# The last phase's down projection by seven block products instead of eight

## The chip, the cores and the metric

The kernel runs on one core of one Trainium2 chip. The metric is device time in microseconds from launch to end; smaller is better.

## The reference, cut to what matters

Four batches ("tiles" here) of 512 tokens, 512 features. Three blocks follow each other, each with a residual:

```
x = x + 0.5 * ffn(layernorm(x))       # hidden 2048
x = x + scan_layer(layernorm(x))      # z = x W^T, gated scan over tokens, 4 decays, layernorm
x = x + 0.5 * ffn(layernorm(x))       # the same ffn weights

ffn(x):  gate = x Wg^T;  up = x Wu^T;  h = silu(gate) * up;  return h Wd^T     # all fp32
```

The down projection `h Wd^T` is [512 tokens x 2048] by [2048 x 512] for each tile.

## The kernel before, in words

**Precision.** Every fp32 product is made of three matmuls in the fp32r format (`three`, L1567 to 1571): both operands are split into a high part (a cast by ACT) and a low part (value minus high part, by DVE), and high x high, high x low and low x high are summed in PSUM.

**Phases.** The eight ffn passes (four tiles, two ffns) are done two at a time, in four phases `p` of two token tiles each, called tile 0 and tile 1 of the phase. Phase 0 also reads and splits all weights and keeps the split ones in DRAM (`gu_kept`, `dn_kept`); later phases fetch them. Phases 1 and 2 carry the scan layer beside them. Phase 3 (`LAST` in the change) only has an ffn.

**Sets.** A phase has 16 sets, one for each hidden tile pair member; gate and up of both token tiles are made by seven products (`prod1` to `prod7`, six matmuls of 512 columns each) of sums of operands, Winograd's form of Strassen's scheme. Over two sets (even, odd) the hidden rows 2q and 2q+1 of tile 0 and tile 1 come out (`gated11`, `gated21`, `gated12`, `gated22`, L1069 to 1096). DVE joins the products (`c11`, `c22`, `c12`, L1048 to 1067); ACT copies partial results out of PSUM and applies silu.

**Down projection.** Tile 0's goes beside the sets: in set si `down0(si - 2)`, half of it (`down0_begin`) after prod6, half (`down0_end`) after prod4; steps 14 and 15 follow set 15. A step is 4 token groups x `three` = 12 matmuls of 512 columns. Tile 1's hidden rows stay in `hid1`, and its 16 steps `down1(p, m)` (L1697) follow in the "window" at the end of the phase, from `zx`, a ring of four rows that `d1_hi` (ACT, L785) and `d1_lo` (DVE, L1321) fill. Weights stand in `dn`, a ring of four (hi and lo of one inner tile, 512 KB), fetched by `fetch_dn` (L426) on SP's queue.

**The order** of every engine is written out by hand; all waits are on semaphores. In phase 0 POOL makes four sums of the gate and up weights of a set (`sums`, L941), ACT and DVE split them (`gu_hi_a`, `gu_lo_a` and so on) and the down weights (`dn_hi_of`, `dn_lo_of`), one set ahead of their use; SP stores them (`keep_a`, `keep_b`, `keep_dn`). In the windows of phases 0 to 2 DVE also normalises and transposes the next phase's input (`norm_x`, `blocks_x`, with POOL's `place_second` and the sums `t_of`, L1462 to 1519), between its `d1_lo` steps.

```
                d1_lo(p, 0)
                d1_lo(p, 1)
                d1_lo(p, 2)          # L1464 to 1466: DVE's window begins
```

**The end.** `add_y1` (DVE, L1333) adds half of each PSUM bank to `x_tok`, and SP stores each 256 KB unit (L570).

Of the kernel before, what the change touches and what calls it, by code (L numbers as in the profile page):

```python
# [44 lines left out]


def macaron_kernel(nc, x_in, w_ffn_in, w_scan_in, lam_logit_in, eta_in, gamma_in, beta_in, out):
# [10 lines left out]
    DN = 4  # L58
    assert tokens == 512 and D == 512 and DT == ST == 4 and HT == 16 and tiles == 4 and K == 4

    with ExitStack() as ctx:
# [10 lines left out]
        xt = sb("xt", [P, 7, 2, 2, tokens], F32R)  # L72
        zx = sb("zx", [P, 2, DT, tokens], F32R)
# [4 lines left out]
        dn = sb("dn", [P, DN, 2, D], F32R)  # L78
# [49 lines left out]
        dn_kept = nc.dram_tensor("dn_kept", [HT, P, 2, D], F32).ap()  # L128
# [9 lines left out]
        d1_ps = [ps_a, ps_b, ps_c, aux]  # L138
        first_turn_ps = [ps_d[0], ps_d[1], ps_d[2], ps_d[3], ps_a, ps_b, ps_d[2], ps_d[3]]
# [131 lines left out]
        zw_loaded = sem("zw_loaded")  # L271
        x_stored = sem("x_stored")
# [18 lines left out]
        d1_last = sem("d1_last")  # L291
        turned_x = sem("turned_x")
# [29 lines left out]
        zw_lo = sem("zw_lo")  # L322
        y0_added, y1_added = sem("y0_added"), sem("y1_added")
# [29 lines left out]
        def _(sp):  # L353
# [120 lines left out]
            for k in range(2, SETS):  # L474
# [32 lines left out]
            keep_dn(15)  # L507
            sp.wait_ge(dn_stored[2], 16 * 4)
# [17 lines left out]
            for p in range(1, PH):  # L526
                for si in range(SETS):
# [18 lines left out]
                    fetch_dn(32 * p + si - 2 + DN)  # L546
                    if g + 2 < SETS * PH:
                        fetch_b(g + 2)
                    if beside and si == 15:
                        load_back(p, 0, 0)  # L550
                        load_back(p, 0, 1)
                for n in range(32 * p + 14, 32 * p + 32):
# [9 lines left out]
                    if p == 2 and m in (8, 10, 12, 14) or p == 3 and m in (4, 6, 8, 10):  # L562
                        sp.wait_ge(y0_added, 4 * p + 4)
                        store_unit(2 * (p - 2), (m - (8 if p == 2 else 4)) // 2)
# [3 lines left out]
            for q in range(ST):  # L568
                sp.wait_ge(y1_added, 4 * (PH - 1) + q + 1)
                sp.dma_start(out_v[3, :, q, :], x_tok[:, 3 * ST + q, :]).then_inc(out_stored, 16)  # L570
            sp.wait_ge(out_stored, 16 * 13)

        @block.scalar
        def _(act):
# [120 lines left out]
            def dn_hi_of(h):  # L695
# [3 lines left out]
                act.copy(dn[:, h % DN, 0, :], dn_raw[:, h % 2, :]).then_inc(dn_hi, 1)  # L699
# [85 lines left out]
            def d1_hi(p, m):  # L785
                wait(act, d_done, 32 * p + 16 + m - 4 + 1 if m >= 4 else 32 * p)
                if m < 4 and p == 0:
                    act.wait_ge(plain_done, 8)
# [3 lines left out]
                act.copy(zx[:, 0, m % 4, :], hid1[:, m, :]).then_inc(d1hi_ready, 1)  # L792

# [64 lines left out]
            for p in range(PH):  # L858
# [3 lines left out]
                for si in range(2, SETS):  # L862
# [45 lines left out]
                g = SETS * p + SETS - 1  # L908
                d1_hi(p, 0)
# [30 lines left out]
        def _(pool):  # L940
            def sums(k):  # L941
# [9 lines left out]
                pool.tensor_tensor(w[:, 7, :], w[:, 4, :], w[:, 1, :], ALU.subtract).then_inc(sums_ready, 1)  # L951

# [58 lines left out]
            for k in range(2, SETS + 1):  # L1011
# [3 lines left out]
                sums(k)  # L1015
                if k == 11:
# [30 lines left out]
        def _(dve):  # L1047
# [21 lines left out]
            def gated11(g):  # L1069
# [4 lines left out]
                dve.tensor_tensor(v, v, sg("11"), ALU.mult).then_inc(hid11_done, 1)  # L1074
# [16 lines left out]
            def gated21(g):  # L1091
# [3 lines left out]
                dve.tensor_tensor(sg("21"), sg("21"), chain_bank(g % SETS)[:, :], ALU.mult  # L1095
# [340 lines left out]
            def one_set(p, si):  # L1436
# [12 lines left out]
                before_c12(p, si)  # L1449
                c12(g)  # L1450
                if up:
                    gated12(g)
                    lo0(g, 1)
# [102 lines left out]
            for p in range(PH):  # L1556
# [6 lines left out]
                window(p)  # L1563

        @block.tensor
        def _(pe):
# [101 lines left out]
            def down0(p, h, q):  # L1668
# [3 lines left out]
                return three(ps_d[q][:, :], hid0[:, h % 2, 0, a], hid0[:, h % 2, 1, a], dn[:, s, 0, :],  # L1672
                             dn[:, s, 1, :], h == 0, h == HT - 1)
# [23 lines left out]
            def down1(p, m):  # L1697
# [4 lines left out]
                for q in range(ST):  # L1702
# [10 lines left out]
                    last = three(d1_ps[q][:, :], zx[:, 0, m % 4, a], zx[:, 1, m % 4, a], dn[:, s, 0, :],  # L1713
# [198 lines left out]
```

## Time and profile before

| | us |
|---|---|
| median of 3 runs (1021.63 to 1021.70) | 1021.67 |
| span of the profiled execution | 1020.2 |
| PE busy in it | 1014.4 |
| DVE / ACT / POOL busy | 671.5 / 408.6 / 162.5 |

The profiled execution's own time is not among the three runs; its span, from first to last instruction, is 1.47 us below their median. Phase 0 ends with its window from about 206 to 255 us, phase 3's last set begins at 955.7 and its window runs to the end. PE's listed durations overlap, since matmuls are pipelined: pace is read from starts. The granted clock of PE is 1.00 in every stretch.

### The profile page before, as it was taken

To read this page: it belongs to the slowest core of one execution; us is meant where nothing else is said; L and a number is where in the kernel's file an instruction comes from. 1 tells how busy PE (TensorE), PEld (TensorE's weight loads), DVE (VectorE), ACT (ScalarE), POOL (GpSimd) and SP (SyncE) were. 2 spreads that over 40 slices of the span, in tenths; PEclk is the share of its full clock that TensorE was granted. 3 is DMA by queue.
4 is the path that set the end of the run, shared out by engine and by line. 5 is a ranking of instruction groups with operands and counts; after the bars stand their busy time and mean duration, and the time that the engine had idled before them with its cause. 6 is when DMAs were issued, how large, how long until landed. Compare 5 with 4: busy or idle time off the path is not lost.

```text
span 1020.2 us, 12550 instructions
## 1 busy us (share of the span) xinstructions
PE 1014.4 (99%) x4508; PEld 841.2 (82%) x4508; DVE 671.5 (66%) x1013; ACT 408.6 (40%) x669; POOL 162.5 (16%) x187
## 2 busy tenths in 40 slices
PE   8999999999999999999999999999999999999998
PEld 8888888888888888888888888888888888888887
DVE  7756665598988687857978877786685333333342
ACT  6645446465433622224732363231382322222311
POOL 4123343125300200210430020021040000000000
PEclk9999999999999999999999999999999999999999
DMA  6588877678667555647856764454677565555265
GB/s 206 224 325 318 301 265 253 252 229 272 242 227 231 182 181 167 200 144 236 270 167 230 235 216 150 146 185 141 228 252 225 207 191 193 204 196 190 85 189 187
DMA packets 61710, 217.89 MB, mean 214 GB/s; under 512 B 6352, under 2 KB 15568, under 8 KB 53968
## 3 DMA queue, kind: packets, MB, share of 16 engines
q1 hardware_dynamic: 61072, 216.03, 62.8%
q10 hardware_dynamic: 576, 1.05, 0.3%
q8 instruction: 36, 0.59, 0.2%
q14 instruction: 26, 0.21, 0.1%
HBM read 170.92 MB, written 46.14 MB: 213 GB/s over the span
## 4 chain that ended last, share of the span: by engine, by line
PE 99%; DVE 1%; DMA 0%; POOL 0%; ACT 0%; issue 0%; DVEq 0%; ACTq 0%
PE ps_a L1569 8%; PE ps_a L1571 8%; PE ps_a L1570 8%; PE ps_b L1569 8%; PE ps_b L1571 8%; PE ps_b L1570 8%; PE ps_c L1569 7%; PE ps_c L1571 7%; PE ps_c L1570 7%; PE ps_d L1569 7%; PE ps_d L1571 7%; PE ps_d L1570 7%; PE aux L1569 3%; PE aux L1571 3%; PE aux L1570 3%; PE ps_d L1731 1%
## 5 line engine op out<-in xcount | busy, mean ns | idle before, releaser
L1060 DVE TENSOR_TENSOR tmp<-tmp,ps_c 128x512 f32<-128x512 f32 x59 | 40.4, 685 | 138.9 <-PE ps_c L1571 138.9
L1569 PE MATMUL ps_a<-xt,gu 128*128 128x512 f32 x304 | 118.3, 389 | 0.0
L1570 PE MATMUL ps_a<-xt,gu 128*128 128x512 f32 x304 | 118.3, 389 | 0.0
L1571 PE MATMUL ps_a<-xt,gu 128*128 128x512 f32 x304 | 118.3, 389 | 0.0
L1570 PE MATMUL ps_b<-xt,gu 128*128 128x512 f32 x286 | 111.3, 389 | 0.0
L1571 PE MATMUL ps_b<-xt,gu 128*128 128x512 f32 x286 | 111.3, 389 | 0.0
L1569 PE MATMUL ps_b<-xt,gu 128*128 128x512 f32 x286 | 111.3, 389 | 0.0
L1571 PE MATMUL ps_d<-dn,hid 128*128 128x512 f32 x256 | 99.6, 389 | 0.0
L1569 PE MATMUL ps_d<-dn,hid 128*128 128x512 f32 x256 | 99.6, 389 | 0.0
L1570 PE MATMUL ps_d<-dn,hid 128*128 128x512 f32 x256 | 99.6, 389 | 0.0
L1570 PE MATMUL ps_c<-xt,gu 128*128 128x512 f32 x236 | 91.8, 389 | 0.0
L1571 PE MATMUL ps_c<-xt,gu 128*128 128x512 f32 x236 | 91.8, 389 | 0.0
L1569 PE MATMUL ps_c<-xt,gu 128*128 128x512 f32 x236 | 91.8, 389 | 0.0
L1260 DVE TENSOR_TENSOR_SCAN hid<-lam,h_t 128x512 f32<-128x512 f32 x64 | 76.5, 1217 | 1.1
L1067 DVE TENSOR_TENSOR tmp<-tmp,ps_c 128x512 f32<-128x512 f32 x59 | 40.2, 682 | 50.7 <-PE ps_c L1571 50.0
L587 ACT COPY tmp<-ps_a 128x512 f32<-128x512 f32 x28 | 16.4, 587 | 128.1 <-PE ps_a L1571 127.9
L1571 PEld LDWEIGHTS ps_a<-xt,gu 128*128 128x128 f32 x304 | 57.1, 188 | 11.9
L1570 PEld LDWEIGHTS ps_a<-xt,gu 128*128 128x128 f32 x304 | 57.1, 188 | 11.9
L1569 PEld LDWEIGHTS ps_a<-xt,gu 128*128 128x128 f32 x304 | 57.0, 188 | 11.8
L1102 DVE TENSOR_TENSOR hid<-tmp,hid 128x512 fp32r<-128x512 f32 x59 | 40.6, 688 | 36.0 <-ACT hid L644 35.9
L1571 PEld LDWEIGHTS ps_b<-xt,gu 128*128 128x128 f32 x286 | 53.7, 188 | 11.2
L1570 PEld LDWEIGHTS ps_b<-xt,gu 128*128 128x128 f32 x286 | 53.7, 188 | 11.1
(207 smaller groups left out, 2113.7 us busy)
## 6 DMA issues: line engine op xcount, KB each, us to landing
dn<-dn_kept SPq DMA_DIRECT2D x112, 512.0 KB, 3.7
gu<-gu_kept SPq DMA_DIRECT2D x46, 1024.0 KB, 5.0
gu<-gu_kept SPq DMA_DIRECT2D x46, 768.0 KB, 5.6
gu_kept<-gu SPq DMA_DIRECT2D x14, 1024.0 KB, 4.4
gu_kept<-gu SPq DMA_DIRECT2D x14, 768.0 KB, 4.2
dn_kept<-dn SPq DMA_DIRECT2D x16, 512.0 KB, 5.1
h_t<-w_ffn_in SPq DMA_DIRECT2D x18, 256.0 KB, 4.8
x_tok<-w_ffn_in SPq DMA_DIRECT2D x18, 256.0 KB, 5.1
```

Source lines behind the costliest of these rows:

```text
L587: act.copy(p1s(si), chain_bank(si)[:, :]).then_inc(p1_copied, 1)
L1060: dve.tensor_tensor(dst, u3s(si), p5_bank(si)[:, :], ALU.add).then_inc(c22_done, 1)
L1067: dve.tensor_tensor(dst, u2s(si), p5_bank(si)[:, :], ALU.add).then_inc(c12_done, 1)
L1102: dve.tensor_tensor(hid0[:, odd, 1, :], v, hid0[:, odd, 0, :].bitcast(F32), ALU.subtract).then_inc(lo0_ready, 1)
L1260: return dve.tensor_tensor_scan(scan_row(j, k), lam[:, k:k + 1].to_broadcast([P, tokens]), h_t[:, j % 4, :], 0.0, ALU.mult, ALU.add)
L1569: pe.matmul(dst, a_hi, b_hi, start=start, stop=False, skip_group_check=chained)
L1570: pe.matmul(dst, a_hi, b_lo, start=False, stop=False, skip_group_check=chained)
L1571: return pe.matmul(dst, a_lo, b_hi, start=False, stop=stop, skip_group_check=chained)
L1731: last = pe.matmul(dst[:, c], w[:, k * P:(k + 1) * P], x[:, k, c], start=w_part == x_part == 0 and j == k == 0 and c.start == 0, stop=x_pa ...
```

## The change: what it does

In phase 3 the two tiles' down projections become one block product. Inner tiles are taken in pairs (even, odd), the output features in halves of 256, the two token tiles are the other block index. Seven products of 256 columns stand for eight.

- `first_block(q, odd)`: tile 0's hidden row 2q + odd against the first 256 features of its weights; twelve matmuls of 256 columns, into `x_ps` (even) or `y_ps` (odd), in place of the down0 half step after prod6. The half step after prod4 is gone in phase 3. The last two, q = 7, follow set 15.
- `batch(w, i)`: five products Q5, Q6, Q3, Q7, Q4, each in four batches of 24 matmuls. Their operands are sums of hidden rows (`s_of` on DVE, four operations of 128x512 per pair), split by `stage_hi_of` (ACT) and `stage_lo_of` (DVE), 128x1024 each, into the seven `xt` slots as the sets leave them. `add_product` on DVE adds the PSUM banks to `x_tok` after each product (two blocks of 128x2x256).
- Sums of the down weights are made in phase 0: `t_sums_of` (POOL, four of 128x256 per pair), `t_hi_of`, `t_lo_of` (128x1024), from and into parts of `zx`, and stored by `keep_t` in `t_kept` (1 MB per pair, two DMAs with pieces of 1 KB).
- `dn` and `dn_kept` keep hi and lo of each half of 256 side by side; the matmuls of the other phases read the same 512 columns in two pieces.
- Hidden rows of tile 0 stay in free buffers in phase 3 (`first_row`), for s_of.

Core of the diff:

```diff
 def load_dn_raw(h):
     wait(sp, dn_lo, h - 1)
+    wait(sp, t_sums, 4 * (h // 2))
...
+def keep_t(j):
+    sp.wait_ge(t_lo, j + 1)
+    for part in range(2):
+        sp.dma_start(t_kept[j, :, :, part], t_part(part).bitcast(F32)).then_inc(t_stored, 16)
...
 # SP, phase 0, set k:
+    if k >= 4 and k % 2 == 0:
+        keep_t(k // 2 - 2)
+keep_t(6)
 sp.wait_ge(dn_stored[0], 16 * 4)
 fetch_dn(16)
...
 fetch_dn(17)
 keep_dn(15)
+keep_t(7)
 sp.wait_ge(dn_stored[2], 16 * 4)
 fetch_dn(18)
...
 # ACT
+def t_hi_of(j):
+    act.wait_ge(t_sums, 4 * j + 4)
+    if j == 0:
+        act.wait_ge(plain_done, 8)
+    wait(act, t_stored, 32 * j)
+    act.copy(t_part(0), t_raw(j)).then_inc(t_hi, 1)
 def d1_hi(p, m):
     wait(act, d_done, 32 * p + 16 + m - 4 + 1 if m >= 4 else 32 * p)
-    if m < 4 and p == 0:
-        act.wait_ge(plain_done, 8)
+    if m < 2 and p == 0:
+        act.wait_ge(t_lo, PAIRS)
+    if 2 <= m < 4 and p == 0:
+        act.wait_ge(t_stored, 32 * PAIRS)
...
     dn_hi_of(si)
+    if si % 2 == 0:
+        t_hi_of(si // 2 - 1)
+    if si == 15:
+        t_hi_of(7)
...
 # POOL
     sums(k)
+    if k % 2 == 0 and k <= SETS:
+        t_sums_of(k // 2 - 1)
...
 # DVE, before c12 of set si in phase 0
     dn_lo_of(si)
+    if si % 2 == 0:
+        t_lo_of(si // 2 - 1)
+    if si == 15:
+        t_lo_of(7)
...
 # DVE, phase 3: s_of(si // 2 - 1) between c11 and c22 of even sets; after set 15:
+stage_lo_of(1)
+s_of(PAIRS - 1)
+stage_lo_of(2)
+for b in range(2):
+    add_block(x_ps, b, 2, 0, first_done, 2 * PAIRS - 1)
+stage_lo_of(3)
+for b in range(2):
+    add_block(y_ps, b, 2, 0, first_done, 2 * PAIRS, b + 1)
+stage_lo_of(4)
+for n in range(5, 20):
+    stage_lo_of(n)
+    if n % 4 == 1:
+        add_product(n // 4 - 1)
+add_product(Q4)
...
 # PE
+def first_block(q, odd):
+    n = SEG + q
+    if odd == 0:
+        pe.wait_ge(dn_loaded[n % DN], 16 * dn_loads(n))
+    pe.wait_ge(lo0_ready, 16 * LAST + 2 * q + odd + 1)
...
+    for t in range(ST):
+        a = slice(t * P, (t + 1) * P)
+        last = three(unit_half(y_ps if odd else x_ps, t), hid0[:, odd, 0, a], hid0[:, odd, 1, a],
+                     dn[:, n % DN, odd, 0, :], dn[:, n % DN, odd, 1, :], q == 0 and t % 2 == 0,
+                     q == PAIRS - 1, True)
+    last.then_inc(first_done, 1)
+
+def batch(w, i):
+    m = 4 * w + i
+    n = SEG + PAIRS + m
+    banks = z_ps if w in (Q5, Q3) else x_ps
+    pe.wait_ge(dn_loaded[n % DN], 16 * dn_loads(n))
+    pe.wait_ge(stage_lo, m + 1)
...
+    if i == 0 and w != Q5:
+        pe.wait_ge(block_added, {Q6: 2, Q3: 6, Q7: 8, Q4: 12}[w])
+    op = stage_op(m)
+    for b in range(2):
+        for k in range(2):
+            for t in (2 * b, 2 * b + 1):
+                a = slice(t * P, (t + 1) * P)
+                last = three(unit_half(banks, t), xt[:, op, 0, k, a], xt[:, op, 1, k, a],
+                             dn[:, n % DN, k, 0, :], dn[:, n % DN, k, 1, :],
+                             w == Q5 and i == k == 0 and t % 2 == 0, i == 3 and k == 1, True)
+        if b == 0 and i == 3:
+            last.then_inc(bank_done, 1)
+    last.then_inc(batch_done, 1)
...
 # PE, phase 3, set si
     prod6(g)
-    down0_begin(p, si - 2)
+    first_block((si - 2) // 2, si % 2)
     prod7(g)
     prod5(g)
     prod4(g)
-    down0_end(p, si - 2)
     prod3(g)
...
-for h in (14, 15): ...      # phase 3: down0 14 and 15, down1 0 to 15
+for odd in range(2):
+    first_block(PAIRS - 1, odd)
+for w in (Q5, Q6, Q3, Q7, Q4):
+    for i in range(4):
+        batch(w, i)
```

The output of the phase is stored in a tile of 1 MB once ten blocks are added, half a tile at twelve, and two units of 256 KB after the last two.

## Rows read from the trace of the kernel before

**Rows 1.** The page: engines (busy us, share, instructions), and a group of weight loads.

```profile
PE 1014.4 (99%) x4508; PEld 841.2 (82%) x4508; DVE 671.5 (66%) x1013; ACT 408.6 (40%) x669; POOL 162.5 (16%) x187
...
L1571 PEld LDWEIGHTS ps_a<-xt,gu 128*128 128x128 f32 x304 | 57.1, 188 | 11.9
```

**Rows 2.** The page: the chain that ended last, by engine.

```profile
PE 99%; DVE 1%; DMA 0%; POOL 0%; ACT 0%; issue 0%; DVEq 0%; ACTq 0%
```

**Rows 3.** Timeline of PE, phase 0's window (start us, duration us, instruction): down0(15), down1(0), down1(14).

```profile
208.95 0.39 PE L1569 MATMUL ps_d<-dn,hid 128*128 128x512 f32 x1
...
211.67 0.39 PE L1569 MATMUL ps_a<-dn,zx 128*128 128x512 f32 x1
...
249.75 0.39 PE L1569 MATMUL ps_a<-dn,zx 128*128 128x512 f32 x1
```

**Rows 4.** Timeline of PE at the start: 256 columns, then 128-column transposes.

```profile
11.16 0.76 PE L1731 MATMUL ps_a<-xt,gu 128*128 128x256 f32 x5
...
10.97 3.11 PE L1731 MATMUL ps_a<-xt,gu 128*128 128x256 f32 x24
...
22.10 1.03 PE L1781 MATMUL ps_d<-ident,hid 128*128 128x128 f32 x8
22.89 0.48 PE L1731 MATMUL ps_d<-xt,zx 128*128 128x512 f32 x1
```

**Rows 5.** Instructions of L1731 (duration ns least/median/most, first and last start).

```profile
L1731 PE MATMUL ps_a<-xt,gu x24: 281/283/356, 11.0 to 13.8; 128*128 128x256 f32 x24
```

**Rows 6.** Timeline, a set of phase 0: last sum on POOL, the cast that reads it.

```profile
103.30 0.73 POOL L951 TENSOR_TENSOR x_tok<-x_tok 128x256 f32<-128x256 f32 x1
...
110.40 1.05 ACT L654 CAST gu<-x_tok 128x1024 fp32r<-128x1024 f32 x1
```

**Rows 7.** Stretches (busy by engine, granted clock, DMA share, GB/s).

```profile
60.00:150.00 90.00, 90.00 (x398) 74.51 (x397) 55.34 (x80) 45.17 (x73) 29.38 (x32) 1.00 0.86 313
...
208.00:209.00 1.00, 1.00 (x6) 0.81 (x6) 1.00 (x2) 0.00 (x0) 0.00 (x0) 1.00 0.89 365
209.00:210.00 1.00, 1.00 (x6) 0.84 (x5) 1.00 (x3) 0.00 (x0) 0.00 (x0) 1.00 0.03 12
```

**Rows 8.** DMA issues from 60 to 75 us (KB each, us to landing).

```profile
x_tok<-x_in SPq DMA_DIRECT2D x1, 1024.0 KB, 8.0
```

**Rows 9.** Timeline of DVE, end of phase 0's sets and its window.

```profile
205.69 0.69 DVE L1153 TENSOR_TENSOR dn<-gb,dn 128x512 fp32r<-128x512 f32 x1
206.50 0.69 DVE L1067 TENSOR_TENSOR tmp<-tmp,ps_c 128x512 f32<-128x512 f32 x1
...
207.83 0.69 DVE L1102 TENSOR_TENSOR hid<-tmp,hid 128x512 fp32r<-128x512 f32 x1
208.43 1.89 DVE L1323 TENSOR_TENSOR zx<-hid,zx 128x512 fp32r<-128x512 f32 x3
...
235.11 1.80 DVE L1211 TENSOR_TENSOR hid<-tmp 128x1024 f32<-128x1024 f32 x1 [0.58 <-POOL tmp L968]
...
247.09 1.22 DVE L1204 TENSOR_TENSOR xt<-hid,xt 128x1024 fp32r<-128x1024 f32 x1
248.23 0.68 DVE L1323 TENSOR_TENSOR zx<-hid,zx 128x512 fp32r<-128x512 f32 x1
```

**Rows 10.** Timeline, phase 3's last set: prod5's last matmul, c22, gated21, hi0.

```profile
963.60 0.39 PE L1571 MATMUL ps_c<-xt,gu 128*128 128x512 f32 x1
...
964.09 0.69 DVE L1060 TENSOR_TENSOR tmp<-tmp,ps_c 128x512 f32<-128x512 f32 x1 [4.03 <-PE ps_c L1571]
...
965.90 0.68 DVE L1095 TENSOR_TENSOR tmp<-tmp,ps_b 128x512 f32<-128x512 f32 x1
...
966.74 0.62 ACT L644 CAST hid<-tmp 128x512 fp32r<-128x512 f32 x1 [2.92 <-PE ps_d L1571]
```

**Rows 11.** Timeline, the end: PE's last matmul and DVE's last add.

```profile
1016.64 0.39 PE L1571 MATMUL aux<-dn,zx 128*128 128x512 f32 x1
1017.06 0.69 DVE L1341 SCALAR_TENSOR_TENSOR x_tok<-aux,x_tok 128x512 f32<-128x512 f32 x1
```

More of the change, by code:

```diff
@@ L44 @@
 B11, B21, T2, T3, T1, T4, B22 = range(7)
+Q5, Q6, Q3, Q7, Q4 = range(5)
 def macaron_kernel(nc, x_in, w_ffn_in, w_scan_in, lam_logit_in, eta_in, gamma_in, beta_in, out):
@@ L72, in macaron_kernel @@
         xt = sb("xt", [P, 7, 2, 2, tokens], F32R)
+        with nc.sbuf_tensor("zx_rows", [P, 2 * DT, tokens], F32) as zx_rows:
+            pass
         zx = sb("zx", [P, 2, DT, tokens], F32R)
@@ L240, in first_sg, with by_half, t_raw, t_part @@
             return hid1[:, {"11": 8, "21": 9, "12": 10, "22": 11}[name], :]
+        def by_half(row):
+            return row.rearrange("p (a n) -> p a n", a=2)
+        def t_raw(j):
+            r = 4 * (j % 2)
+            return zx_rows[:, r:r + 2, :].rearrange("p r (a n) -> p (r a) n", a=2)
+        def t_part(part):
+            return zx[:, part, 2:4, :].rearrange("p r (a n) -> p (r a) n", a=2)
+        def first_rows(i, odd):
+            if i == 0:
+                return h_t[:, 2 * odd:2 * odd + 2, :]
+            if i == 1:
+                return zw[:, :, :].bitcast(F32) if odd else gb[:, :, :]
+            r = 4 * odd + 2 * (i - 2)
+            return x_tok[:, r:r + 2, :]
+        def first_row(q, odd):
+            return first_rows(q // 2, odd)[:, q % 2, :]
+        def stage_rows(w, i):
+            return {Q5: hid1[:, 4 * i:4 * i + 3:2, :], Q6: zx_rows[:, 2 * i:2 * i + 2, :], Q3: first_rows(i, 1),
+                    Q7: first_rows(i, 0), Q4: hid1[:, 4 * i + 1:4 * i + 4:2, :]}[w]
+        def stage_op(n):
+            return STAGES[n % len(STAGES)]
         def row_x(k, r):
@@ L271, in macaron_kernel @@
         zw_loaded = sem("zw_loaded")
+        t_stored = sem("t_stored")
         x_stored = sem("x_stored")
@@ L322, in macaron_kernel @@
         zw_lo = sem("zw_lo")
+        t_lo = sem("t_lo")
+        s_step = sem("s_step")
+        stage_lo = sem("stage_lo")
+        block_added = sem("block_added")
         y0_added, y1_added = sem("y0_added"), sem("y1_added")
@@ L567, in _ @@
                     store_tile(1)
[L568 to L571, printed above, removed]
+            for n in range(SEG + PAIRS + DN - 1, SEG + PAIRS + 20):
+                fetch_dn(n)
+            sp.wait_ge(block_added, 10)
+            store_tile(2)
+            sp.wait_ge(block_added, 12)
+            sp.dma_start(out_v[3, :, :, HALF:D], x_tok[:, 12:16, HALF:D]).then_inc(out_stored, 16)
+            for b in range(2):
+                sp.wait_ge(block_added, 13 + b)
+                sp.dma_start(out_v[3, :, 2 * b:2 * b + 2, 0:HALF], x_tok[:, 12 + 2 * b:14 + 2 * b, 0:HALF]
+                             ).then_inc(out_stored, 16)
+            sp.wait_ge(out_stored, 16 * 9)
         @block.scalar
@@ L908, in _ @@
                 g = SETS * p + SETS - 1
+                if p == LAST:
+                    stage_hi_of(0)
+                    hi0(g, 1)
+                    for n in range(1, 20):
+                        stage_hi_of(n)
+                    break
                 d1_hi(p, 0)
@@ L1156, in zw_lo_of, with add_product @@
+            def add_product(w):
+                banks, tile, half, added = {Q5: (z_ps, 3, 1, 0), Q6: (x_ps, 2, 1, 0), Q3: (z_ps, 2, 1, 8),
+                                            Q7: (x_ps, 3, 1, 6), Q4: (x_ps, 3, 0, 0)}[w]
+                add_block(banks, 0, tile, half, bank_done, w + 1, added)
+                add_block(banks, 1, tile, half, batch_done, 4 * w + 4, added)
             def zw_lo_of(j):
@@ L1364, in after_c11 @@
                     gu_lo_a(si + 1)
+                if p == LAST and si % 2 == 0:
+                    s_of(si // 2 - 1)
                 if p in (1, 2):
@@ L1449, in one_set @@
                 before_c12(p, si)
+                if p == LAST and si == SETS - 1:
+                    lo0(g, 1)
+                    stage_lo_of(0)
                 c12(g)
@@ L1452, in one_set @@
                     gated12(g)
-                    lo0(g, 1)
+                    if p < LAST or si < SETS - 1:
+                        lo0(g, 1)
             def decays():
```

152 lines of the change are left out of this document (130 added, 22 removed).

## The prediction

> **What bounds the kernel now.** The page's first part comes first: TensorE (PE) is busy for 1014.4 of 1020.2 us, VectorE (DVE) for 671.5 [rows 1]. PE ends are modelled there, so the chain of waits comes next: 99% of the span runs through PE [rows 2]. The kernel is a stream of matmuls with no hole after the start, so only two things can move its end: the time that PE's instructions take, and a hole that the change opens. DVE's 66% says nothing by itself; how far it runs ahead of PE must be read at each place that the change touches.
>
> **What PE gains.** In the last phase 16 `down0` and 16 `down1` steps issue 2 x 16 x 4 x 3 = 384 matmuls of 512 columns. After the change seven block products stand in their place: `first_block` is called 16 times with 12 matmuls each (192), `batch` 20 times with 24 (480): 672 of 256 columns. That is 336 in units of 512, seven eighths of 384.
>
> The pace is read from starts, not from durations. A `down0` step of 12 matmuls takes 211.67 - 208.95 = 2.72 us, 0.2267 us each [rows 3]; the listed 0.39 us overlap. 256-column matmuls stand in the trace before once, in `plain_first`: five of them last 0.76 us together and one alone 0.283, so four steps take 0.477 us, 0.119 each; all 24 last 3.11, so 23 steps take 2.83, 0.123 each, with the waits for their operands inside [rows 4, 5]. At a granted clock of 1.00 (the 2.4 GHz level) 512 columns need 213.3 ns and 256 need 106.7, so 0.2267 and 0.120 carry the same fixed 13.3 ns. I take 0.120. Before: 384 x 0.2267 = 87.0 us. After: 672 x 0.120 = 80.6. **PE gains 6.4 us**, of the 10.2 by which the columns alone shrink (48 x 213.3 ns); 288 more instructions x 13.3 ns = 3.8 us go to fixed parts. With 0.119 and 0.123 as ends the gain is 7.1 to 4.4.
>
> Every matmul loads its own weights, and with 256 columns there is half the time to hide that. The row of 128-column transposes bounds it: eight follow each other in 22.89 - 22.10 = 0.79 us, 0.099 each [rows 4], so one load with its matmul can be done each 0.10 us, below 0.120. The Trainium skill ("TensorE: Matmul & The Clock Gate", LDWEIGHTS) says that a load takes the number of weight columns over 1.2 GHz, whatever the moving width: an estimate from it is 107 ns, longer than the 106.7 ns in which 256 columns stream, and unhidden it would make 672 x (107 + 107) = 143 us of the down projection. By that rule the change loses. The trace agrees that the load is near the limit, and shows it hidden: 0.12 us, not 0.21.
>
> **Phase 0: the price of the sums of the weights.** Per pair of inner tiles POOL makes four sums of 128x256 (0.73 us each), ACT one cast of 128x1024 (1.05), DVE one subtraction of 128x1024 (1.22) [rows 6, 9], and SP two stores, 1.05 MB, of `t_kept`; eight pairs.
> - In the sets this lies beside PE. POOL ends `sums` at 104.03 and ACT reads them at 110.40 [rows 6]: 6.4 us of slack, and the new sums stand behind those of their own set. DVE's new 1.22 us stands before `c12`, whose result PE needs only at the next set's `prod5`. DMA moves 313 GB/s from 60 to 150 us at a busy share of 0.86, and 365 when packed; 8 x 1.05 MB over some 170 us add 49 GB/s: 362, at that limit [rows 7]. A stage load can fall behind one store, 1.05 / 0.365 = 2.9 us, less than the 6.4. I take 0, between 0 and 3.
> - At the end of the phase it doesn't. `t_lo_of(7)` goes ahead of DVE's `c12` of set 15. Before, `dn_lo_of(15)` starts at 205.69 and its successor could start 0.60 later, at 206.29; c12 did at 206.50 [rows 9]. With 1.13 us more (successors start 0.09 ahead of the listed end) c12 starts at 207.42, 0.92 late, and `lo0(15, 1)` ends at 207.83 + 0.69 + 0.92 = 209.44. PE wants it at 208.95, when `down0(15)` starts [rows 3]: 0.5 us of stall. ACT's `d1_hi(0)` now waits for `t_lo` (207.5) ahead of `hi0(15, 1)`, which ends by 208.7: just in time.
> - Then the main cost. `d1_hi(2)` of phase 0 waits for `t_stored` 256: the last pair's two stores, because it overwrites their source in `zx`. SP issues them behind `keep_dn(15)` once t_lo_of(7) has ended, at 207.5 and 207.9. The DMA engines are busy with earlier transfers until 209.0 (365 GB/s from 208 to 209, 12 in the next microsecond [rows 7]), and 1.05 MB at 0.365 MB/us take 2.87 us: landed at 212.1 or so, with 0.2 for the completion. ACT casts for 0.62, so DVE's `d1_lo(2)` starts at 212.8. Before, it was the third of three from 208.43, 0.60 apart: 209.63 [rows 9]. **DVE is 3.2 us late**, and everything queued behind it (norm_x, the 32x32 transposes, the sums for the next phase) shifts with it, because DVE has no reserve there: its longest gap up to 249 us is the 0.58 before 235.11 [rows 9], in which it waits for POOL's twelve copies, and these start when DVE's last transpose is done, so they shift too.
> - PE feels it where its lead is thinnest. `d1_lo(14)` ends at 248.23 + 0.68 = 248.91, `down1(14)` starts at 249.75 [rows 3, 9]: 0.84 us. PE ends up 3.2 - 0.84 = **2.4 us late**, the 0.5 of above included, since the later need swallows it. Ends: 0.5 if the stores cost DVE nothing beyond the 0.92 (PE's lead of 0.84 and the first 0.5 cover it), 6.2 if the second takes the 8.0 us of the slowest 1 MB transfer [rows 8] (landed 215.9, DVE 7.0 late).
>
> **Phase 3.** Beside the sets `first_block` (12 x 0.12 = 1.44 us between prod6 and prod7) replaces 2 x 1.36. What shrinks is the stretch between prod5 and prod3, from 2.72 to 1.36 us, in which c22 must be done. PE's last matmul of prod5 starts at 963.60, its slot ends at 963.83, c22 starts at 964.09 [rows 10]: 0.26 + 0.69 = 0.95 of 1.36. No stall. `s_of` puts four DVE operations of 0.69 between c11 and c22 of the even sets, where DVE has an idle stretch before c22 (4.03 us in the set shown [rows 10]): 0.
> - Last set: c22, lo0, gated22, gated21 start 0.60 apart, so gated21 ends 965.90 + 0.68 = 966.58 [rows 10], 2.75 us after prod5's end. hi0 (0.62) and lo0 (0.69) follow, ending 4.06 after prod5; first_block(7, 1) can start 1.36 + 1.36 + 1.44 = 4.16 after it. Before, two more half steps gave 2.7 us of room. I take 0.1 here and at the third batch (its staging waits behind s_of(7) and ends as the second batch does), up to 1.
> - Batches: 2.88 us of PE each against 1.05 of ACT and 1.22 of DVE, staged seven ahead. Hidden. The `dn` fetch is 512 KB per 2.88 us, with three batches to land. Hidden.
> - Q7 to Q4: both sum into x_ps, and Q4's first matmul waits until DVE has read the last half of Q7. From the slot end 1016.87 (1016.64 + 0.23) DVE starts 0.19 later and works 0.69 [rows 11]; PE follows: **0.95 us** of hole, between 0.88 and 1.2.
> - The tail stays: one DVE add and one store of 256 KB after the last matmul; 0, within 0.3.
>
> **Sum.** 6.4 - 2.4 - 0.95 - 0.1 = 2.95 us less: the profiled execution's span would go from 1020.2 to 1017.25 us. The median shown, 1021.67, lies 1.47 above the span, and keeps to it: **1018.7 us**.
>
> **Rivals.**
> - *The window hides the stores* (their landing costs DVE nothing beyond its 0.92): 6.4 - 0.5 - 0.95 - 0.1 = 4.85, 1016.8. For it: the DMA engines are all but idle after 209 [rows 7]. Against: 1.05 MB alone take 2.87. Chance 0.15.
> - *The stage loads of phase 0 come late*: one store of 1.05 MB stands ahead of a load where the queue is full already, once or in several sets, and PE waits for 2.9 us more, the one store's time: 2.95 becomes 0.05, 1021.6. For it: 362 of 365 GB/s. Against: 6.4 us of slack. Chance 0.15.
> - *The last pair's store lands late, and the end is slower than before*: place and price as above, d1_hi(2) on ACT. At 8.0 us DVE is 7.0 late, PE 6.2: 6.4 - 6.2 - 1.05 = -0.85, 1022.5. It decides from a landing at 215.1, where the stall passes 5.35 us, 7.2 us after the second issue. For it: the 8.0 of [rows 8]. Against: the engines are at 12 GB/s just after 209. Chance 0.1.
> - *The weight load sets the pace* of 256-column matmuls: with the 0.188 us of PEld's rows [rows 1] each, 672 x 0.188 = 126 us, 39 more than 87.0, and with the 3.45 of waits 1064. Break-even at (87.0 - 3.45) / 672 = 0.1243. Against: 0.119 to 0.123 in the very trace. Chance 0.03.
> - The forecast itself has 0.52 (1018.0 to 1019.6); 0.05 for holes not seen, worth 1 to 3 us.
>
> What this kernel's measurement can tell from no change is about 0.2%, 2.04 us: below 1019.63 is faster, above 1023.71 slower. The forecast clears this by 0.9 us only, so a stall of 3.3 us instead of 2.4 in the window makes it "same". Faster 0.48 + 0.15 = 0.63; same: 0.15 + 0.04 + some 0.08 of the late store and the unseen = 0.27; slower 0.10. The range, 1016.6 to 1021.6, holds the forecast, the hidden store and the late stage loads' price.
>
> **What would show it.** In the trace after: `first_block` and `batch` matmuls start 0.120 us apart (0.124 and more would sink the gain). SP's two stores to `t_kept` issued near 207.5; ACT's idle time ahead of d1_hi(2), released by DMA, ends at 212; d1_lo(2) starts near 212.8; PE idles 0.5 us before down0(15) and in sum 2.4 us by the start of phase 1, with the waits named d1_lo. No PE idle time before 200 us. In phase 3 none up to set 15; 0.95 us before Q4 on DVE's add. Wrong would be: PE waiting within the sets of phase 0 (DMA), c22 as PE's releaser in phase 3, or phase 1 starting as early as before.

## The result and the profile after

The changed kernel takes 1024.18 us (median of 8 runs, 1023.85 to 1025.08); the kernel before takes 1021.63 beside it (8 runs, 1021.58 to 1021.71). The ratio is 1.0026, 95% interval [1.0016, 1.0036]: 2.55 us slower, where 1018.7 was forecast, and outside the range. The profiled execution took 1023.93 us; its span, from first to last instruction, is 1022.2.

The page of the changed kernel, engines and chain by engine (columns as in [rows 1, 2]):

```profile
PE 1010.2 (99%) x4796; PEld 849.0 (83%) x4796; DVE 720.5 (70%) x1063; ACT 426.6 (42%) x681; POOL 193.1 (19%) x219
```

```profile
PE 92%; DVE 3%; DMA 2%; issue 1%; ACT 1%; SPq 1%; POOL 0%; DVEq 0%; ACTq 0%
```

PE has 4 us less work and 288 more instructions than in [rows 1]. But the chain of waits, 99% PE in [rows 2], now leaves PE for DVE, ACT, DMAs and SP's queue. The view of waits names the places. Its columns are the waiting tile and line, the releaser (what ended the wait), then us in total, times, longest. Of the lines named, L1507 is `d1_lo`, L680 and L707 are ACT's copies of products out of PSUM, L1248 is the split of `hid0`, L1330 the addition of a product to `x_tok`:

```profile
PE ps_a L1779 <- DVE zx L1507: 2.2, 2, 1.1
PE ps_d L2036 <- ACT hid L782: 1.7, 1, 1.7
PE ps_b L1977 <- POOL ident L1148: 1.6, 1, 1.6
PE ps_b L1779 <- ACT tmp L680: 1.3, 1, 1.3
PE ps_d L1779 <- DVE x_tok L1330: 0.9, 1, 0.9
PE ps_a L1779 <- ACT tmp L707: 0.6, 1, 0.6
PE ps_d L1779 <- DVE hid L1248: 0.5, 1, 0.5
```

Those for POOL ident and ACT hid L782 lie before the first product and were there before (1.6 and 1.1). The other five are new. By the starts each of them costs PE 0.15 to 0.35 us more than the idle time listed, and so the loss is measured here by the starts of the same matmul in both traces. The best mark is phase 1's first product. Timeline of PE before, and after:

```profile
255.19 0.39 PE L1569 MATMUL ps_a<-xt,gu 128*128 128x512 f32 x1
```

```profile
261.79 0.39 PE L1779 MATMUL ps_a<-xt,gu 128*128 128x512 f32 x1
```

**Phase 0 became 6.60 us longer; from this mark to the end of the span it takes 1022.2 - 261.79 = 760.4 us instead of 1020.2 - 255.19 = 765.0.** The rest gained 4.6 us, and phase 0 took that and 2 us more.

*The pace* came as forecast. Timeline of PE in the last phase, product Q7: starts 0.12 us apart.

```profile
1005.12 0.28 PE L1780 MATMUL ps_d<-dn,xt 128*128 128x256 f32 x1
1005.24 0.28 PE L1781 MATMUL ps_d<-dn,xt 128*128 128x256 f32 x1
```

*Q7 to Q4*, DVE and PE together (in brackets: idle time before, and its releaser). PE's last start in Q7 is 1005.96, its slot ends at 1006.08, the next product starts 1.04 later; 0.95 was forecast.

```profile
1006.28 0.69 DVE L1330 SCALAR_TENSOR_TENSOR x_tok<-ps_d,x_tok 128x512 f32<-128x512 f32 x1 [0.74 <-PE ps_d L1781]
...
1007.12 0.35 PE L1779 MATMUL ps_d<-dn,xt 128*128 128x256 f32 x1 [0.88 <-DVE x_tok L1330]
```

*Phase 0 loses at four places.* Between the marks that surround each, PE's starts fall behind those of before by 0.79 us at 43.8, 1.60 at 76.7, 0.64 at 212.1 and 2.80 at 227.1 and 231.2, with some 0.7 in small pieces. Their rows, first the start of the phase. POOL ends the first pair's sums with the row at 24.67; the four behind it are the sums of set 3, and DVE's subtractions lie beside them:

```profile
24.67 0.74 POOL L1092 TENSOR_TENSOR zx_rows<-gb,zx_rows 128x256 f32<-128x256 f32 x1
25.37 0.74 POOL L1072 TENSOR_TENSOR x_tok<-x_tok 128x256 f32<-128x256 f32 x1
26.07 1.72 POOL L1073 TENSOR_TENSOR x_tok<-x_tok 128x256 f32<-128x256 f32 x1
27.75 1.72 POOL L1075 TENSOR_TENSOR x_tok<-x_tok 128x256 f32<-128x256 f32 x1
29.55 1.07 POOL L1077 TENSOR_TENSOR x_tok<-x_tok 128x256 f32<-128x256 f32 x1
...
24.62 0.68 DVE L1295 TENSOR_TENSOR hid<-hid,ps_d 128x512 f32<-128x512 f32 x1
...
27.22 1.65 DVE L1398 TENSOR_TENSOR hid<-tmp,hid 128x1024 f32<-128x1024 f32 x1
28.79 1.23 DVE L1248 TENSOR_TENSOR hid<-hid 128x512 fp32r<-128x512 f32 x1
29.94 1.76 DVE L1400 TENSOR_TENSOR hid<-tmp 128x1024 f32<-128x1024 f32 x1
...
42.58 0.63 ACT L713 ACTIVATE tmp<-tmp 128x512 f32<-128x512 f32 x1 [2.72 <-DVE tmp L1196]
...
43.83 0.47 PE L1779 MATMUL ps_a<-xt,gu 128*128 128x512 f32 x1 [0.57 <-ACT tmp L707]
```

The same forms take 0.74 us on POOL, and 1.22 and 0.68 on DVE, where they run alone: both engines slow down while they work at the same time. DVE's row at 24.62, which reads one of its two inputs from PSUM, does not. Before, `sums(3)` was over at 25.4. Now `t_sums_of(0)` stands ahead of it in POOL's queue. DVE is still late at 42.58, where ACT gets its operand 1.5 us later than before (41.04), and through ACT's queue PE is late at 43.83 (43.03 before).

Then sets 4 and 5: a load of 1 MB, the two stores of pair 0 right behind it, ACT's split of pair 1, and PE.

```profile
62.94 1.57 SPq L570 DMA_DIRECT2D x_tok<-x_in  x1
64.55 1.47 SPq L469 DMA_DIRECT2D t_kept<-zx  x2
...
75.06 1.04 ACT L802 CAST zx<-zx_rows 128x1024 fp32r<-128x1024 f32 x1 [3.91 <-DMA t_kept<-zx]
...
76.65 0.50 PE L1779 MATMUL ps_b<-xt,gu 128*128 128x512 f32 x1 [1.26 <-ACT tmp L680]
```

Last the window, which answers to [rows 3, 9]:

```profile
210.04 1.24 SPq L469 DMA_DIRECT2D t_kept<-zx  x2
...
212.08 0.47 PE L1779 MATMUL ps_d<-dn,hid 128*128 128x512 f32 x1 [0.48 <-DVE hid L1248]
...
215.86 1.14 ACT L897 CAST zx<-hid 128x512 fp32r<-128x512 f32 x2 [4.15 <-DMA t_kept<-zx]
...
216.51 0.69 DVE L1507 TENSOR_TENSOR zx<-hid,zx 128x512 fp32r<-128x512 f32 x1 [3.37 <-ACT zx L897]
...
227.07 0.47 PE L1779 MATMUL ps_a<-dn,zx 128*128 128x512 f32 x1 [1.10 <-DVE zx L1507]
231.20 0.47 PE L1779 MATMUL ps_a<-dn,zx 128*128 128x512 f32 x1 [1.13 <-DVE zx L1507]
```

The chain of waits runs through the second of these stores, and through the second store of pair 0. The two are the longest pieces of the whole chain (start, us, what):

```profile
65.30 9.69 DMA t_kept<-zx
210.60 5.23 DMA t_kept<-zx
```

And the stretches of that window (columns as in [rows 7], which ended at 210): the DMA engines are full.

```profile
210.00:211.00 1.00, 1.00 (x7) 0.81 (x6) 0.96 (x3) 0.96 (x2) 0.00 (x0) 1.00 0.99 389
...
212.00:213.00 1.00, 0.92 (x4) 0.81 (x5) 1.00 (x2) 0.00 (x0) 0.00 (x0) 1.00 1.04 349
213.00:214.00 1.00, 1.00 (x6) 0.80 (x5) 0.14 (x1) 0.00 (x0) 0.00 (x0) 1.00 1.02 355
```

### The profile page after: what moved, and what is told of

It is laid out like the page before. It is cut to its first block, busy times and chain, and to the rows that moved or that the text cites. A ratio compares the mean times of both kernels' runs of the same rounds, so it can differ in the third digit from the quotient of the medians.

```text
span 1022.2 us, 13275 instructions
## 1 busy us (share of the span) xinstructions
PE 1010.2 (99%) x4796; PEld 849.0 (83%) x4796; DVE 720.5 (70%) x1063; ACT 426.6 (42%) x681; POOL 193.1 (19%) x219
## 3 DMA queue, kind: packets, MB, share of 16 engines
q10 hardware_dynamic: 576, 1.05, 0.3%
## 4 chain that ended last, share of the span: by engine, by line
PE 92%; DVE 3%; DMA 2%; issue 1%; ACT 1%; SPq 1%; POOL 0%; DVEq 0%; ACTq 0%
PE ps_a L1779 8%; PE ps_a L1780 8%; PE ps_a L1781 8%; PE ps_b L1779 7%; PE ps_b L1780 7%; PE ps_b L1781 7%; PE ps_d L1779 7%; PE ps_d L1781 7%; PE ps_d L1780 7%; PE ps_c L1781 6%; PE ps_c L1780 6%; PE ps_c L1779 6%; PE aux L1779 3%; PE aux L1780 3%; PE aux L1781 3%; DMA t_kept<-zx 1%
## 5 line engine op out<-in xcount | busy, mean ns | idle before, releaser
L1779 PE MATMUL ps_d<-dn,hid 128*128 128x512 f32 (+1 forms) x256 | 92.9, 363 | 0.5 <-DVE hid L1248 0.5
L1781 PE MATMUL ps_d<-dn,hid 128*128 128x512 f32 (+1 forms) x256 | 92.8, 363 | 0.0
L1780 PE MATMUL ps_d<-dn,hid 128*128 128x512 f32 (+1 forms) x256 | 92.8, 362 | 0.0
L680 ACT COPY tmp<-ps_a 128x512 f32<-128x512 f32 x28 | 16.4, 587 | 118.3 <-PE ps_a L1781 118.2
L1779 PEld LDWEIGHTS ps_b<-xt,gu 128*128 128x128 f32 x286 | 53.7, 188 | 12.6 <-ACT tmp L680 1.7
L1781 PEld LDWEIGHTS ps_b<-xt,gu 128*128 128x128 f32 x286 | 53.7, 188 | 11.2
L1780 PEld LDWEIGHTS ps_b<-xt,gu 128*128 128x128 f32 x286 | 53.7, 188 | 10.8
```

The lines of the kernel that those rows point to most:

```text
L680: act.copy(p1s(si), chain_bank(si)[:, :]).then_inc(p1_copied, 1)
L1779: pe.matmul(dst, a_hi, b_hi, start=start, stop=False, skip_group_check=chained)
L1780: pe.matmul(dst, a_hi, b_lo, start=False, stop=False, skip_group_check=chained)
L1781: return pe.matmul(dst, a_lo, b_hi, start=False, stop=stop, skip_group_check=chained)
```

## The experiments

The theory: the last phase does about what was computed for it, and phase 0 loses its 6.6 us at these places, each by the order of the work and not by its amount. All kernels below start from the changed one. The kernel before took 1021.70 to 1021.74 (medians) beside them; "phase 0" is the start of phase 1's first product in each trace, against 255.19 before and 261.79 after.

**The last pair's parts in other buffers.**

```diff
+            if j == 7:
+                last = gb[:, :, :].bitcast(F32R) if part else zw[:, :, :]
+                return last.rearrange("p r (a n) -> p (r a) n", a=2)
...
                 if 2 <= m < 4 and p == 0:
-                    act.wait_ge(t_stored, 32 * PAIRS)
+                    act.wait_ge(t_stored, 32 * 7)
```

(Its two stores count on a semaphore of their own, which the loads of gamma and beta and the batches' first fetch wait for; ACT and DVE write the two buffers once their last users are done.)

> The last pair's parts of the T sums go to two other buffers (zw and the raw down rows), so ACT's first split rows of down1 need not wait until the pair's two stores have landed; nothing else is changed. Theory (the window of phase 0 lost about 3.5 us to this wait: ACT's split of row 2 begins 215.86, 4.15 us after the one before): down1(2) to down1(5) no longer come late, the waits on DVE zx (2.2 us of PE's) go, and the time falls from 1024.2 to 1020.7 (1020.2 to 1021.4). Rival (the added sums and stores themselves, the engines' work and the transfers beside down0(14) to down1(5), make the window late, whichever buffer they use): the waits stay on PE and the time stays within 0.5 us of 1024.2.

Measured: 1020.93 us (11 runs, 1020.66 to 1023.68), 3.25 less, ratio to before 0.9995 [0.9986, 1.0004]. Phase 0 ends at 258.51, 3.28 earlier. The stores are issued at almost the same time, 210.10 for 210.04, and the same loads follow them, but ACT's splits for down1(1) to (3) now run together and no wait on DVE zx is left in PE's list:

```profile
210.11 0.62 ACT L906 CAST zx<-hid 128x512 fp32r<-128x512 f32 x1 [3.91 <-DVE gb L1315]
210.64 0.62 ACT L746 CAST hid<-tmp 128x512 fp32r<-128x512 f32 x1
211.16 1.66 ACT L906 CAST zx<-hid 128x512 fp32r<-128x512 f32 x3
```

The wait for the landing was the cost. The stores and loads themselves cost PE nothing there: from `down0(15)` to the mark it falls back by 0.03 us more.

**The pairs' stores a set earlier.**

```diff
-                if k >= 4 and k % 2 == 0:
-                    keep_t(k // 2 - 2)
+                if k >= 3 and k % 2:
+                    keep_t((k - 3) // 2)
 
-            keep_t(6)
```

> The two stores of each pair of T sums are issued in the odd steps of the loader's loop, a step after the pair is finished, instead of a set and a half behind it. Theory (the single staging buffer: ACT's split of pair 1 waits 3.91 us for the store of pair 0, which is issued 16 us after the pair was ready, and PE loses 1.3 to 1.6 us at 76.65): the stop goes and the time falls from 1024.2 to 1022.6 (1022.2 to 1023.2). Rival (the DMA engines are full at 60 to 110 us, share 0.96, and a store issued earlier lands no earlier or pushes a stage load late): the same stop, within 0.4 us of 1024.2, or a new one on PE behind a late stage.

Measured: 1022.75 (11 runs, 1022.49 to 1023.39), 1.43 less. The first stores go out at 53.64 instead of 64.55, ACT's splits of the pairs wait for no store, and PE's wait on `tmp` L680 has gone from its list. Phase 0 ends at 260.58, 1.21 earlier: the window's two stops are 2.5 us here, not 2.2. The edit does two things at once: it issues pair 0's stores 11 us earlier, and so ahead of the 1 MB load that stood before them.

**Q4 waits bank by bank.**

```diff
-                    pe.wait_ge(block_added, {Q6: 2, Q3: 6, Q7: 8, Q4: 12}[w])
+                    pe.wait_ge(block_added, {Q6: 2, Q3: 6, Q7: 8, Q4: 11}[w])
...
+                    if b == 1 and i == 0 and w == Q4:
+                        pe.wait_ge(block_added, 12)
```

> Between the last two products the engine waits only for the addition of the first bank (11), and for the second (12) ahead of its own matmuls. Theory (the end's only stop, 0.88 us of idle at 1007, is the second of two additions in a row): the idle falls to what the first addition takes, 0.1 us or nothing is left, and the time falls by 0.9 to 1.0 us to 1023.2. Rival (DVE's additions and splits are what is late, the product's first split rows among them): the stop moves to the next wait and the time falls by less than 0.3 us.

Measured: 1023.59 (11 runs, but from 1021.86 to 1024.44), 0.59 less, where 0.9 to 1.0 was expected. The median alone would leave it open. The trace doesn't: Q4's first matmul (1007.09) starts 0.12 us behind Q7's last, and DVE's second addition only starts after it,

```profile
1006.97 0.28 PE L1781 MATMUL ps_d<-dn,xt 128*128 128x256 f32 x1
1007.09 0.28 PE L1779 MATMUL ps_d<-dn,xt 128*128 128x256 f32 x1
...
1007.29 0.69 DVE L1330 SCALAR_TENSOR_TENSOR x_tok<-ps_d,x_tok 128x512 f32<-128x512 f32 x1 [0.75 <-PE ps_d L1781]
```

and from the mark to the end it is 1022.1 - 262.78 = 759.3 us, 1.1 less than the 760.4 of after. What hid it in the profiled execution is phase 0, which the edit doesn't touch and which took 0.99 us longer: PE's stop in set 5 was 2.00 us instead of 1.26, the landing ahead of it 0.6 later, and the window's two stops were 2.6 us for 2.2.

**No sums of the weights at all.** The kernel leaves out the sums, their splits and stores; the batches fetch kept down rows of the same size, and so multiply by other weights.

```diff
-                if k % 2 == 0 and k <= SETS:
-                    t_sums_of(k // 2 - 1)
...
-                        if si % 2 == 0:
-                            t_hi_of(si // 2 - 1)
...
-                    if si % 2 == 0:
-                        t_lo_of(si // 2 - 1)
...
-                        kept = t_kept[2 * i:2 * i + 2, :, c].rearrange("j p t n -> p j t n")
+                        kept = dn_kept[4 * i + c // 2:4 * i + 4:2, :, c % 2].rearrange("h p t n -> p h t n")
```

> Phase 0 forms, splits and stores no sums of down rows, and the batches of the end fetch kept down rows of the same size in their place (the output is not the reference's: two of the last tiles get products with other weights). What is left of the change is the last phase alone. Theory (the last phase gained 4.77 us and phase 0 lost 6.60 by the starts of the same products in both traces): 1024.2 - 6.6 = 1017.6 (1017.2 to 1018.3). Rival (the last phase owes part of its gain to a phase 0 that ran late, or the loss of phase 0 is partly the new layout of the down rows, which stays): 1019 to 1021.

Measured: 1017.45 (5 runs, 1017.11 to 1017.47). Phase 0 ends at 255.22 against 255.19 before: the whole loss belongs to the sums and what they bring, none to the new layout of the down rows, and the last phase owes nothing to phase 0 (1015.6 - 255.22 = 760.4, as after).

**The sums without their stores.** The sums are made and split, but neither stored nor used.

```diff
-                wait(act, t_stored, 32 * j)
+                wait(act, t_lo, j)
                 act.copy(t_part(0), t_raw(j)).then_inc(t_hi, 1)
...
-            keep_t(7)
```

> The sums of the down rows are formed and split as in the changed kernel (32 operations of GpSimd, 8 of ACT, 8 of DVE), but not stored, nothing waits for a store, and the batches of the end fetch other kept rows of the same size (the output is not the reference's). It stands between the changed kernel (1024.2) and the one without sums (1017.45). Theory (5 of the 6.6 us that phase 0 lost are waits for two landings in the one staging buffer, the rest is engine time: 0.8 at 43.83 and 0.64 at 212.08): 1017.45 + 1.4 = 1018.9 (1018.4 to 1019.5). Rival (the engines' work is the larger part, the waits only show where it comes out): 1021 or more.

Measured: 1019.05 (8 runs, 1018.94 to 1019.17). So of 6.7 us between the kernels with and without sums, 5.1 hang on stores and what waits for them, 1.6 on the engines' work. Of the four waits in phase 0 the two expected ones are left:

```profile
PE ps_a L1770 <- ACT tmp L700: 0.6, 1, 0.6
PE ps_d L1770 <- DVE hid L1239: 0.5, 1, 0.5
```

**The first pair's sums behind those of set 3.**

```diff
                     pool.wait_ge(xlo_ready, parts(0, T4))
+                    t_sums_of(0)
                 sums(k)
-                if k % 2 == 0 and k <= SETS:
+                if k % 2 == 0 and 2 < k <= SETS:
```

> The first pair's four sums move on GpSimd from behind the kernel's sums of set 2 to ahead of those of set 4, so that the sums of set 3 start 2.9 us earlier and no longer run beside DVE's four sums over x. Theory (the stop of 0.57 us and the 0.79 us of the start come from DVE operations that grow from 1.22 to 1.76 us beside GpSimd's): the stop at 43.8 goes, DVE's four operations return to 1.22 to 1.3 us, and the time falls by 0.5 to 0.8 to 1023.5. Rival (DVE's start is late for another reason, such as the rows' landing): the four operations stay at 1.3 to 1.8 us and the time stays within 0.3 us of 1024.2.

Measured: 1023.93 (9 runs, 1023.24 to 1025.96), 0.25 less: a miss in the time, and by the time alone the rival (within 0.3 us of 1024.2) would have it. But the mechanism did what the theory said. DVE's operations are back at 1.22 us and the wait at 43.8 has gone. The gain ends in set 5:

```profile
74.93 1.05 ACT L802 CAST zx<-zx_rows 128x1024 fp32r<-128x1024 f32 x1 [4.50 <-DMA t_kept<-zx]
...
76.52 0.50 PE L1780 MATMUL ps_b<-xt,gu 128*128 128x512 f32 x1 [1.85 <-ACT tmp L680]
```

PE arrives there earlier and waits 1.85 instead of 1.26 us, for a landing that came at 74.9 instead of 75.05: the store is issued at 64.66, not earlier than the 64.55 of the changed kernel. (This profiled execution is the 1025.96 one; its window was slower as well.)

**The first three edits together.**

> The edits of the first three runs together: the last pair in other buffers, the pairs' stores a step behind the sums, the last product's wait bank by bank. Theory (three separate stops on PE's path; alone they took 3.25, 1.43 and 0.6 to 1.0 off 1024.2): they add up, 1024.2 - 5.3 to 5.7 = 1018.7 (1018.2 to 1019.3), faster than before by 3 us. Rival (phase 0's loss moves from one stop to the next, since the two stops of phase 0 share the full DMA engines and the single buffer): 1020 or more.

Measured: 1018.36 (5 runs, 1017.96 to 1018.41), ratio to before 0.9967 [0.9954, 0.9979]. Alone the three took 3.25, 1.43 and 0.59, together 5.82: more than the sum by 0.5, which is about what the trace found for the third beyond its median.

**With it, the first sums later, or set 15 reordered, or both.** The reorder, on ACT (DVE's splits move likewise, ahead of c22):

```diff
+                    if p == 0 and si == 15:
+                        dn_hi_of(si)
+                        t_hi_of(7)
                     copy_u3(g)
```

> The three mended waits (1018.36 together) and the first pair's sums moved behind those of set 3, without the new order of set 15. With the two stops on landings out of the way, the move has nothing behind it that can take its gain back; alone it brought 0.25 us in the medians, though the stop at 43.8 had gone from the trace. Theory: 1018.36 - 0.8 = 1017.6 (1017.3 to 1017.9). Rival (the 0.8 at the start are swallowed by a later need anyway): 1018.2 or more.

> The three mended waits (1018.36 together) and, of the two further edits that brought 1016.53, only the order of set 15 of phase 0: the splits of the last down row and the last pair ahead of the set's last ones. Theory (the 1.83 us between those two kernels are two separate stops, 0.79 at the start and 0.7 to 1.1 at down0(15) with what follows in the window): 1018.36 - 1.0 = 1017.3 (1017.0 to 1017.6). Rival (one of the two edits brings it all): 1016.5 or 1018.3.

> As the run of the three edits, and the first pair's sums later, and in set 15 of phase 0 the splits of the last down row and the last pair go ahead of the set's last products' sums, since ACT and DVE otherwise issue them between those and the split of hid0 that down0(15) waits for. Theory (0.79 us at the start and 0.64 at down0(15) are the engine time that is left): 1018.7 - 0.6 to 1.3 = 1017.8 (1017.3 to 1018.4). Rival (moved ahead, the splits of DVE, 0.69 and 1.23 us, delay the sum for the set's silu instead, and the stop only moves into set 15): as e8 less 0.6 at most, 1018.2 or more.

Measured: first sums later 1017.37, set 15 reordered 1017.38, both **1016.53** (5 runs, 1016.09 to 1016.67; ratio to before 0.9949 [0.9936, 0.9961]). That is 0.99, 0.98 and 1.83 under the three edits: two separate stops, as the theory had it. Both single edits came out inside their ranges. The last one beats the kernel before by 5.2 us and the changed one by 7.7. It is also 1.3 us under the 1017.8 that I expected of it: the move and the reorder brought 1.8 where 0.6 to 1.3 stood. Its waits on PE are the two before the first product that were always there:

```profile
PE ps_d L2053 <- ACT hid L787: 1.6, 1, 1.6
PE ps_b L1994 <- POOL ident L1158: 1.6, 1, 1.6
```

All eight pairs are still summed, split and stored in it, and its chain is PE for 99% again. By mark and rest, in us:

| kernel | median | phase 0 | against 255.19 | from there to the end |
|---|---|---|---|---|
| before | 1021.63 | 255.19 | | 765.0 |
| changed | 1024.18 | 261.79 | +6.60 | 760.4 |
| last pair elsewhere | 1020.93 | 258.51 | +3.32 | 760.5 |
| stores earlier | 1022.75 | 260.58 | +5.39 | 760.4 |
| Q4 by banks | 1023.59 | 262.78 | +7.59 | 759.3 |
| no sums | 1017.45 | 255.22 | +0.03 | 760.4 |
| sums, no stores | 1019.05 | 256.86 | +1.67 | 760.4 |
| first sums later | 1023.93 | 263.78 | +8.59 | 760.4 |
| three edits | 1018.36 | 257.17 | +1.98 | 759.4 |
| three, first sums | 1017.37 | 256.27 | +1.08 | 759.5 |
| three, set 15 | 1017.38 | 256.05 | +0.86 | 759.5 |
| all | 1016.53 | 255.28 | +0.09 | 759.5 |

After the change the last column has two values, 760.4 and 759.4, within 0.1. Everything that differs between these kernels but the 1.0 of Q4 happens ahead of the mark.

The 765.0 of the kernel before needs a caution. Every run on record lies 1.73 to 1.85 us above its own span, and the kernel before has spans of 1019.9 to 1020.0 in the median beside the edits. Its profiled execution, with 1020.2, was about 0.3 us slower than that. In medians the last phase alone gains 1021.70 - 1017.45 = 4.25 us (the kernel without sums), where the starts give 4.6. Which stretch holds the 0.3 no row says.

## Why the prediction was wrong

The prediction had 6.4 - 2.4 - 0.95 - 0.1 = 2.95 us less. Measured by starts it is 4.77 less in the last phase up to PE's end, 6.60 more in phase 0, and 0.1 to 0.2 more behind PE: 2.0 more. Step by step:

- **PE's pace: right.** 0.120 us, as taken, not the 0.124 that would sink it.
- **The last phase: right in kind, 0.6 short.** Forecast 6.4 - 1.05 = 5.35, measured 4.77. Q7 to Q4 took 1.04 for 0.95, the first_block behind the sets about 0.2 for 0.1, the third batch 0.13 within the same 0.1; the other 0.3 is about what is lost right behind each `first_block` of the sets: the next few matmuls of 512 columns start up to 0.236 us apart (808.61, 808.84, 809.08, 809.31) where 0.2267 was taken, some 0.37 us in sum over the 14 blocks. Why, no run shows.
- **"In the sets I take 0": the step that failed.** 2.4 us were lost there, and neither cause was the one that the prediction priced, a stage load that comes late: PE never waited for that. The first is a wait that I listed for the last pair only: `t_hi_of(j)` waits for `t_stored` 32*j, since `zx` holds one pair, so each pair's split waits for the stores before it to land, and ACT's `copy_p1` of the next set stands behind. SP issues these stores only in the next even step of its loop; the second needs 9.7 us from issue to landing, and ACT goes on at 75.06. It is the only pair that stops PE: the second stores of the later pairs land within 6.5 us. Two things are there for it, the DMA engines, at a share of 0.96 from 60 to 110 us, and the 1 MB load of `x_tok` that SP issued just before, at 62.94, and that landed at 71.09; its 8.0 us stood in [rows 8]. With the stores issued 11 us earlier, ahead of that load, nothing waits (1.43 us gained); which of the two counts more no run separates. The second is at the start: I took DVE and POOL durations from rows where each ran alone. POOL's slack was there in set 3 too (its sums end at 30.62, ACT reads them at 37.15); what it did not cover is that DVE's own work, which PE needs at 43.8, takes longer beside POOL's sums. Moving the sums gave 0.99 once nothing stood behind.
- **The window: right mechanism, wrong size.** Named were the wait (d1_hi(2) for the last pair's two stores), its place, and DVE's lateness; the run without the wait gained 3.28. Forecast 2.4, measured 0.64 + 3.5 = 4.14. Two terms were off. The second store landed 5.23 us after its issue, not 4.2, for which the likely reason is that the DMA engines were not idle. I had read the stretches of before only to 210, where they moved 12 GB/s; had I gone on, I would have found the loads of the next down rows and of stage 17, which SP issues right behind the stores, now beside them in the same engines:

```profile
210.00:211.00 1.00, 1.00 (x7) 0.81 (x6) 0.90 (x3) 0.00 (x0) 0.00 (x0) 1.00 0.80 201
211.00:212.00 1.00, 1.00 (x6) 0.84 (x5) 1.00 (x2) 0.00 (x0) 0.00 (x0) 1.00 0.95 368
```

  No run moved these loads alone, so that stays argued. The late landing makes DVE 4.4 late instead of 3.2 (216.51, less the 2.46 by which everything was already late, against 209.63). And the lead that PE spends was taken at `down1(14)`, 0.84; what is late by 4.4 stops PE first at down1(4) and (5). The last 0.3 of the 4.14 I can't derive from DVE's lateness of 4.7 less 0.84 at the end of the window.
- **set 15, down0(15): right.** 0.5 forecast, 0.48 idle and 0.64 in starts. But "included, since the later need swallows it" was not: the two add.
- **The rivals.** "The last pair's store lands late" had the right place and the sign, at 1022.5 and with a chance of 0.1; by its own rule (it decides from a stall of 5.35 us) the window of 4.14 would not have sufficed. Without the 2.4 us in the sets, the time would have been 1021.8, "same". The weight load never showed. The Trainium skill ("TensorE: Matmul & The Clock Gate", LDWEIGHTS) gives a load a time by its own columns alone, an estimate of 107 ns here. The trace lists more, 0.192 us for each load beside 256 columns, and yet a pace of 0.120 (672 matmuls): the loads overlap and none of their time shows.

The sizes close: the forecast span of 1017.25, plus 6.60 - 2.4 = 4.2, plus 5.35 - 4.77 = 0.58, plus 0.17 at the tail, is 1022.2, the span measured (the 0.17 is by spans as the page rounds them). The median stands 2.0 above that span instead of the 1.47 carried over: 0.25 because this profiled execution lay under its median, and the other 0.3 because the 1.47 was too small. It set the median beside the span of a slower execution; a run's own time is 1.73 to 1.85 above its span.

## What to carry to other kernels

When work is added beside a full engine, list every wait that the new code contains, in each turn of its loop and not only the last: a staging buffer with one place turns the landing of a store into a wait of the engine that fills it, and through that engine's queue into a hole in PE. Price a landing by what the DMA queues will hold then, not by how idle they were before the change, and ask first where in its queue the store stands. What an edit gains at one stop can be lost again at the next one, if that is tied to a landing, so mend those first and judge the others by the start of a fixed matmul, not by the median alone.

## What the hardware showed that I had not expected

- **DVE and POOL slow each other.** A 128x1024 subtraction on DVE takes 1.22 us alone and 1.65 to 1.76 beside POOL's sums, a 128x512 one 1.23 for 0.68, while POOL's 128x256 ones take 1.72 for 0.74. With POOL's sums moved, all returned to 1.22 or 1.23 and 0.69 in all three kernels that do so. The Trainium skill ("SBUF — State Buffer", SBUF: two separate sides) says that a DVE operation with two SBUF inputs and a GpSimd operation that reads SBUF take the same pair of ports, one excluding the other. The rows agree on which operations suffer, the unharmed one with a PSUM input too; whether one waits for the whole of the other they don't decide. I had not weighed that rule when I took 1.22 for granted, and the trace of before has a sign of it, a sum on POOL that takes 1.19 us for 0.74 beside such a DVE operation:

```profile
20.34 0.70 DVE L1153 TENSOR_TENSOR dn<-gb,dn 128x512 fp32r<-128x512 f32 x1
...
20.46 1.19 POOL L949 TENSOR_TENSOR x_tok<-x_tok 128x256 f32<-128x256 f32 x1
```

- **A full queue is no bound by itself.** I had taken 365 GB/s for the limit. The kernel with all edits moves more from 60 to 110 us, and PE has no hole in it (same columns as [rows 7]):

```profile
60.00:110.00 50.00, 50.00 (x223) 41.39 (x222) 36.82 (x44) 26.48 (x41) 24.74 (x25) 1.00 1.02 382
```

- **The time of a kernel whose PE waits for a landing scatters more.** The kernel before ranges over 0.6 us in 27 runs, the one without stores over 0.2 in 8. The four that keep the wait in set 5 range over 1.2 in 8 (changed), 3.0 in 11 (last pair elsewhere), 2.6 in 11 (Q4 by banks) and 2.7 in 9 (first sums later). The one that keeps only the wait in the window ranges over 0.9 in 11, those that keep neither over 0.4 to 0.6 in 5 each. So it goes with the wait in set 5 above all; no run was made to test it.
